# Attention outputs in 32x32 tiles: each product of 256 columns made as two of 128

## What is computed

```python
def linear_attention(x, Wq, bq, Wk, bk, Wv, bv, g, bb):
    q = gelu(x @ Wq + bq) + 0.21
    k = gelu(x @ Wk + bk) + 0.21
    v = x @ Wv + bv
    q_r = rope(q)
    k_r = rope(k)
    q, k, v, q_r, k_r = map(to_h, (q, k, v, q_r, k_r))
    kmean = jnp.mean(k, axis=2, keepdims=True)
    z = 1.0 / (jnp.einsum('bhnd,bhmd->bhnm', q, kmean) + 1e-06)
    kv = jnp.einsum('bhnd,bhne->bhde', k_r, v) / n
    out = jnp.einsum('bhnd,bhde->bhne', q_r, kv) * z
    ...
    return layernorm(out + x, g, bb)
```

## Time and profile before

| | |
|---|---|
| median of 3 runs | 1833.14 us (1832.21 to 1834.62) |
| the profiled execution | 1829.56 us |
| its span, first to last instruction | 1827.8 us |
| PE busy | 1806.2 us (99%), 19196 MATMULs and as many weight loads |
| DVE, ACT, POOL busy | 1455.7, 936.8, 1016.6 us |
| TensorE clock granted | 0.998 of 2.4 GHz |
| `outputs` (L934) | 4096 MATMULs and 4096 loads in 32 stages, from 187 us to 985 us |

### The profile page before, as it was taken

One profiled execution on the slowest core, in us unless ns is written; L12 is line 12 of the kernel. 1 busy time (PEld: TensorE's weight loads), 2 busy tenths in 40 slices (PEclk: granted clock), 3 DMA queues, 4 the chain that ended last, 5 costly groups with the idle time before them and its releaser, 6 DMA issues.

```text
span 1827.8 us, 46210 instructions
## 1 busy us (share of the span) xinstructions
PE 1806.2 (99%) x19196; PEld 1477.8 (81%) x19196; DVE 1455.7 (80%) x3454; ACT 936.8 (51%) x1741; POOL 1016.6 (56%) x775
## 2 busy tenths in 40 slices
PE   9999999999999999999999999999999999999998
PEld 3336888888888888888887988888888888888887
DVE  3667787888888888888888768888888888888887
ACT  5554776677667776677667742222322232323231
POOL 1557998999999999999985012222222222222221
PEclk9999999999999999999999999999999999999999
DMA  8372210100103210000105931010101010101000
GB/s 294 150 268 111 94 60 3 37 2 2 37 2 106 94 37 3 29 10 3 60 3 197 306 101 35 36 35 29 42 24 47 24 47 24 46 24 44 26 12 24
DMA packets 25234, 115.38 MB, mean 63 GB/s; under 512 B 4480, under 2 KB 5440, under 8 KB 19904
## 3 DMA queue, kind: packets, MB, share of 16 engines
q1 hardware_dynamic: 21104, 89.69, 14.0%
q0 software_dynamic: 1152, 12.58, 2.0%
q10 hardware_dynamic: 2768, 10.15, 1.5%
HBM read 80.95 MB, written 31.46 MB: 62 GB/s over the span
## 4 chain that ended last, share of the span: by engine, by line
PE 96%; DVE 2%; ACT 1%; DMA 1%; issue 1%; POOL 0%; ACTq 0%; SPq 0%; DVEq 0%; POOLq 0%
PE bankC L1450 13%; PE bankC L32 7%; PE bankC L33 7%; PE bankC L34 7%; PE ring L32 6%; PE ring L34 6%; PE ring L33 6%; PE bankC L1449 6%; PE big L934 5%; PE big L34 3%; PE big L33 3%; PE big L32 3%; PE ring L866 3%; PE big L846 3%; PE conv_ps L256 3%; PE hid_ps L245 3%
## 5 line engine op out<-in xcount | busy, mean ns | idle before, releaser
L1450 PE MATMUL bankC<-down,act_hi 128*128 128x512 f32 x992 | 353.1, 397 | 0.0
L1449 PE MATMUL bankC<-down,act_lo 128*128 128x256 f32 x868 | 246.2, 284 | 0.0
L1450 PEld LDWEIGHTS bankC<-down,act_hi 128*128 128x128 f32 x992 | 186.3, 188 | 41.9
L1575 DVE TENSOR_TENSOR act_lo<-gel,act_hi 128x512 fp32r<-128x512 f32 x256 | 210.5, 822 | 8.7
L33 PE MATMUL bankC<-aT_lo,up_hi 128*128 128x512 f32 x512 | 199.6, 390 | 0.0
L32 PE MATMUL bankC<-aT_hi,up_hi 128*128 128x512 f32 x512 | 199.5, 390 | 0.0
L34 PE MATMUL bankC<-aT_hi,up_lo 128*128 128x512 f32 x512 | 199.4, 389 | 0.0
L1529 POOL TENSOR_TENSOR hC<-hC,vecC 128x1024 f32<-128x1024 f32 x16 | 38.7, 2416 | 282.9 <-PE turn L1424 282.9
L1535 POOL TENSOR_TENSOR rstdC<-var_epsC,minus_halfC 128x4 f32<-128x4 f32 x47 | 56.1, 1193 | 249.5 <-DVE var_epsC L1603 249.5
L1449 PEld LDWEIGHTS bankC<-down,act_lo 128*128 128x128 f32 x868 | 164.1, 189 | 1.4
L774 POOL TENSOR_TENSOR kr<-kr,kc 128x512 f32<-128x512 f32 x128 | 161.9, 1299 | 0.0
(11 more groups left out here) (215 smaller groups left out, 5262.3 us busy)
## 6 DMA issues: line engine op xcount, KB each, us to landing
raw_late<-in_AB SPq DMA_DIRECT2D x30, 320.0 KB, 4.0
u<-hA SPq DMA_DIRECT2D x8, 1024.0 KB, 5.0
u_next<-u SPq DMA_DIRECT2D x8, 1024.0 KB, 6.0
hC<-u SPq DMA_DIRECT2D x16, 512.0 KB, 4.0
xC<-in_x SPq DMA_DIRECT2D x16, 512.0 KB, 4.8
out<-w_flat SPq DMA_DIRECT2D x15, 512.0 KB, 2.6
w_flat<-in_AB SPq DMA_DIRECT2D x22, 320.0 KB, 3.7
w_split<-w_parts ACTq DMA_DIRECT2D x4, 1536.0 KB, 5.9
```

The costliest lines, as they stand in the source:

```text
L1449: e.matmul(bank[:, 0:H], a_lo[:, fb, tok], both[k][:, fb, 0, :], start=False, stop=False)
L1450: m = e.matmul(bank[:, :], a_hi[:, fb, tok], both[k][:, fb, :, :].rearrange("p a h -> p (a h)"), start=fb == 0, stop=fb == FB - 1)
L1575: e.tensor_tensor(a_lo[:, fb, :], g, a_hi[:, fb, :].bitcast(F32), ALU.subtract).then_inc(s_act_lo, 1)
```

## The change

In `outputs` a loop over the two halves of the token groups (`a` = 0 and 4, `blocks` = 4 of the 8 groups) is put between the loop over the channel block and the loop over the two pairs. Each product now has 4 x 32 = 128 columns, and there are 128 of them a unit in place of 64: eight rounds of 16 over the tiles. The sum of columns, the results and the waits are the same.

```diff
+                blocks = TILES // 2
                 for db in range(CB):
-                    for wt, q in ((kv, qc), (kv_rot, qs)):
-                        for j in range(QUARTERS):
-                            for i in range(GR):
-                                ch = slice(D * i, D * i + D)
-                                out = big[i][D * j:D * j + D, :].rearrange("p (a d c) -> p a d c", a=TILES, d=CB)[:, :, db, :]
-                                m = e.matmul(out, wt[ch, db, :], quarter(q[ch, db, :], j), start=q is qc, stop=q is qs)
+                    for a in range(0, TILES, blocks):
+                        for wt, q in ((kv, qc), (kv_rot, qs)):
+                            for j in range(QUARTERS):
+                                for i in range(GR):
+                                    ch = slice(D * i, D * i + D)
+                                    out = big[i][D * j:D * j + D, :].rearrange("p (a d c) -> p a d c", a=TILES, d=CB)
+                                    m = e.matmul(out[:, a:a + blocks, db, :], wt[ch, db, :],
+                                                 quarter(q[ch, db, :], j)[:, a:a + blocks, :], start=q is qc, stop=q is qs)
                 m.then_inc(s_out, 1)
```

## The result

| | before | after |
|---|---|---|
| median | 1833.31 us (1832.21 to 1834.62, 4 runs) | 1933.11 us (1931.91 to 1933.80, 4 runs) |
| the profiled execution | 1829.56 us | 1933.35 us |
| its span | 1827.8 us | 1931.5 us |
| mean granted TensorE clock | 0.998 | 0.993 |

The changed kernel takes 1.0542 times as long, 95% interval 1.053 to 1.0555: 99.8 us more by the medians, 103.7 us by the two spans. Forecast was 1927 us, 94 us more.

What follows compares the result with a forecast made beforehand. PE, through its 32 stages of outputs, was taken to bound the kernel. Waves (+25 us) and instruction packets (+69 us, third borders included) gave 94 us over 1833.1: 1927 us, range 1857 to 1955.

Steps and rivals of the forecast that it cites:

- Waves: Outputs stages: products start in waves of 17, 0.43 us each with 128 columns; +0.78 us a stage, +25 us.
- the rule of 64: PE in the outputs: 64 instructions may be on their way, ended in order; with the first tile's run-ahead, 17 products a wave.
- a fixed price for each product: Rival, outputs: 21 ns a MATMUL whatever its size, +86 us, 1919, up to 1945 with the packets; chance 0.05.
- no change: Rival, outputs: a wave shrinks in full with the columns and packets don't matter, 1833 us; chance 0.06.
- Packets: PE's instruction fetch: one packet of 256 ahead, so a stage's second border comes 3.4 to 3.6 us after its first; +69 us.
- early stages: The 24 outputs stages with first border below instruction 193: first border free, the second waited for, +1.75 us each, 42 us.
- the late ones: The 8 outputs stages with first border from instruction 193: gaps at both borders, 7.2 us each, 22 us beyond the waves.
- waves only: Rival, outputs: more than one packet can be fetched ahead, so borders cost what they do today; 1858 us, chance 0.09.
- Third borders: In 5 or 6 stages with first border below 30, another border in the transposes behind comes 0.8 us too early; +5 us.
- the limit at 193: Outputs stages: a first border at instruction 193 or later means a gap already in the kernel before; 8 such stages.
- The clock: Rival, outputs: the granted clock falls to 0.50 after the longer gaps in each stage, 55 us more, 1982; chance 0.05.

Runs made afterwards that it cites:

- e1_half: The changed kernel computing only the first half of the token groups, 64 products of 128 columns a unit; 1812.77 us (one run).
- e2_pairs: The kernel before with j in pairs, so sixteen consecutive products use eight tiles twice instead of sixteen once; 1841.25 us (one run).
- e9_quarter: The changed kernel with four parts in place of two, 256 products of 64 columns a unit; 2220.56 us (one run).
- e6_after_few: The changed kernel with 44 or 45 no-operations on PE ahead of the outputs in six of 32 units; 1911.45 us, 1.0428 times before.
- e8_before_split: The kernel before with the eight transposes that follow the outputs put between the two channel blocks; 1855.75 us, 1.0117 times before.

## Why the prediction was right

**What bounds the kernel.** A stage's loss showed in full at the end: 94.5 us in the stages, 103.7 in the span, and what DVE, ACT and POOL did more was wait, POOL 42.6 us in its row. Nobody else's wait took the place of PE's.

**Waves.** Forecast 0.43 us for 17 products; the loads resume at 0.43 (the window from 414.94), and `e1_half` has 1.84 us for a stage of 64 products. The term of +0.78 us a stage was never seen alone in the changed kernel, since the packets hold its second half. It is shown by `e1_half` for the first 256 instructions and by the rule of 64 that also fits `e2_pairs`; the prediction's picture of whole waves that follow each other was a shortcut, which gave the right sum where every tile is used once a round and failed in `e2_pairs`. The rivals that needed another rule, a fixed price for each product and no change, fell with `e1_half`.

**Packets.** Forecast for the early stages 2.69 + 0.78 + 1.75 = 5.2 us, measured 5.16; for the late ones 7.2, measured 7.27; some 40 gaps, measured 42; 129 packets, measured 130. That it is the fetching and not the number of products that costs this part is shown by the places of the gaps, all at borders, and by three things that leave the products as they are: 45 no-operations take the late stages from 7.27 to 5.1 us, the same ones take the gaps out of the kernel before, and a table's first number puts a gap in all stages or in none. Only one packet is fetched ahead, so "waves only" was wrong. The Trainium skill says in Runtime: NRT & Kernel Launch, Instruction fetch mechanics, that PE holds 2048 instructions and that crossing a block of 256 is mostly hidden; the traces speak against both for such a stage, with some 69 us, the 94.5 less the 25 that were reckoned for the waves. The Trainium skill speaks in the same section, and in Advanced Engine Details and Errata, ISA Cache, of only two lines of 256 instructions, and that agrees with one packet ahead: behind a gap the next packet starts about 1.1 us after instructions flow again.

**Third borders.** Forecast 5 or 6 of 0.8 us, +5; measured 3 of 0.7 to 0.9, +2.4. Two of the five, with the borders at 24 and 26, show no such wait that stands out.

**What the sum lacked**: 104 us in the profiled execution for 94. The waves, the packets and the third borders were the terms; missing were three more.
- The stage with its border at 190 has no gap before, and I counted it with the early ones. It became a late one, 7.20 us: 2 us too few in the sum. The DMA rows of 8 us around it (busy tenths in 40 slices of 0.2 us, the stage beginning at the 21st), before and after:

```profile
DMA  9471720000000000000000000100000003000000
```

```profile
DMA  6104000000000000000000300100000000000000
```

  Before, a packet had come 3.2 us ahead of the stage (among the marks at the left); after, it starts 0.51 us behind its beginning, the mark in the 23rd slice, as in all late stages. The border ahead lies 66 instructions before the stage. With 63 the packet is late in the kernel before too, with 68 it is early in both. Why it jumps by 3.7 us at this point I don't know (in the slower stretches of the changed kernel packets start up to 14 us after the last border, so the border alone doesn't set their start); it is what makes a stage late, and I took only its result, the limit at 193, from the trace.
- The last unit's stage, border 210, was forecast as an early one, +2.5 us, and grew by 6.7. There the instruction packet does not come in its usual 0.85 to 1.1 us. In this stage, which goes ahead of the feed-forward phase, other transfers fill the DMA engines (its queues, 1075.217 to 1084.01: packets, MB, share):

```profile
q1 hardware_dynamic: 308, 1.30, 50.9%
q8 instruction: 2, 0.03, 1.4%
...
1084.01 0.71 PE L936 MATMUL big<-qs,kv_rot 32*32 32x128 f32 x23 [2.49 <-issue]
```

  The second packet started only 6.4 us into the stage, and the clock fell on it. Whether the traffic delayed the packets was not tried.
- The clock, forecast in no stage or in all (55 us), fell in three: some 5.5 us outside the stages, and 1.3 more in the feed-forward phase. The trace of before had gaps of up to 1.1 us (the prediction's 1.2 is what a gap added to its stage) and one wait of 3.3, so how often it falls between them had no answer there. It fell in few of the gaps of the changed kernel and in all stages of `e9_quarter`, so I should have put it at some of the price and not at all or nothing. Even the wait of the earlier trace rows is no sure sign: PE has it, 3.3 to 3.6 us long, in the ten profiles other than `e9_quarter`, and in `e6_after_few` and `e8_before_split` no half clock follows it.

Against these stand 3 us too much for third borders and 1 us for the early stages. A small misreading made no difference: the prediction says that PE waits for no engine in the attention, and the trace of before has two waits for DVE there, 1.4 us at `turn_kv` of the last unit and 0.4 at the first outputs. The range held, and its lower end, 1857, was far too careful: the eight gaps of before had already shown that no second packet arrives.

## What to carry over

Count the instructions that an engine has to be given, not only the work: a stretch of PE's program that passes two borders less than about 3.5 us apart waits at the second one in this kernel, whatever the array could do, and each of the small fp32 products here costs four of them. Before a dense stretch is rewritten, look where the packets of the instruction queue fall in it: a few instructions that do nothing, in the right six places, took the gaps out of this kernel, and in the changed kernel useful work in front of the second border was nearly free. Move a border only after following it through the whole loop, since it stops in the next dense stretch.

## What the hardware showed

- Changing between 128x128 products and 32x32 ones costs some 0.17 us each time: `e8_before_split` has two changes more a unit, and its stretch is 0.34 us longer.
- A no-operation of PE takes time of its own, 0.70 us idle for 45 ahead of a stage, some 16 ns each, and over 20 ns each between projections.
- The second MATMULs of the fp32 products start 0.24 us behind the first ones, after the first MATMULs of up to fifteen later tiles. A count of 64 instructions on the way that includes both and ends in order gives the last starts of three kernels' stages within 0.02 us.
- In 42 gaps of up to 2.5 us the clock fell from 2.4 to 1.2 GHz only three times; with three or four gaps of 1.5 to 3.2 us in a stage of `e9_quarter` it fell in every stage.
- In the kernel before an instruction packet is fetched 3.2 us ahead of a stage when the border before lies 66 instructions ahead of it, and 0.5 us into the stage when it lies 63 ahead; in the changed kernel 66 is late too.
